# Function table loads written ahead of the wait of the activation that needs them

## The chip, the cores and the metric

The kernel runs on one core of a Trainium2 chip. The metric is the device time of one execution in microseconds; for a kernel run several times the median stands. The engines are TensorE (PE; its weight loads are PEld), VectorE (DVE), ScalarE (ACT), GpSimd (POOL) and SyncE (SP, which issues transfers).

## The reference

The reference is one forward pass of a hybrid network on an input of 2 x 512 x 128 elements read as 8 x 256 tokens of 128 channels. Sixteen blocks follow each other, each as `x = x + block(layernorm(x))`:

```
L0: selective scan,  experts (gelu, top 2 of 8),  linear attention (silu),  experts
L1: gated linear attention (sigmoid),  local attention + gelu MLP,  latent attention,  local attention + gelu MLP
L2: selective scan (silu),  experts (silu, top 2 of 8),  attention,  experts
L3: block-sparse attention,  slots,  grouped-query attention (two kinds),  slots
```

What matters for this change is which function each piece needs of ScalarE. Every layer norm needs `1/sqrt`, which the kernel computes as exp(-0.5 ln(v + eps)). Softmaxes need exp. The experts of L0 and the MLPs of L1 need gelu, the scan of L2, the experts of L2 and the linear attention need silu. The gated attention needs sigmoid. A slot block needs, in this order: ln and exp (norm), gelu, exp (softmax over the kept slots), sigmoid and tanh (the two gates and the candidate of a GRU cell), exp (a softmax between slots), ln and exp (norm).

## The kernel before

The 8 x 256 tokens are cut into four streams of 512 columns. Channels lie on the 128 partitions. Each stream runs all sixteen blocks in order, with its own quarter of the scratch space and its own two banks of PSUM; the streams depend on each other only at the start, at the weights' buffers and through the engines that they share.

The program has one instruction sequence per engine. What each stream does on an engine is a Python generator: `pe`, `act`, `dve`, `pool` and `sp` methods of the blocks. A generator yields the key of the event that its next piece waits for, on ScalarE with the function that the piece needs (for instance `yield self["gates"], ACT.Sigmoid`). It is resumed when `Core.run` (line 479) picks it; then it writes the wait and the instructions up to its next yield, and the events it posts get a semaphore count and a modelled time.

`Core.run` is a list scheduler. Each engine has a modelled time `free` at which it is done with what was written so far. Of all generators whose event has been posted, the one with the lowest rank goes next. The rank is a pair: the modelled start, and the event's time. On ScalarE a generator that needs another function table than the modelled one is ranked 500 ns later (`PATIENCE`, line 251), by `Scalar.delay` (line 333). `keep_clock` (line 503) puts extra matmuls into modelled gaps of TensorE. So every modelled time has a say in the order of the instructions on all engines; the order is fixed when the program is built.

A ScalarE function that isn't in the loaded table needs a table load (ACT_TABLE_LOAD in the trace). `Scalar.activation` (line 337) keeps the modelled table: Ln and Exp count as one, every other function as one of its own, and Copy, Identity and Square are in all. Where the modelled table becomes that of Ln and Exp, the kernel writes the load itself at line 342, directly in front of the activation, so behind the wait that was written before it. For all other functions the kernel writes none: the compiler puts in a load directly in front of an activation whose function isn't in the loaded table, and the trace shows it with the activation's line, 346. A wait may be a field of the instruction that waits, or an instruction of its own in front of it.

Some pieces name the function at the first of two waits. In the experts' silu step (lines 1426 to 1429):

```
e.wait_ge(*(yield self["up", i], ACT.Silu))
if i >= 2:
    e.wait_ge(*(yield self["down", i - 2]))
e.activation(self.h[i % 2][:, 0:width], self.a[:, 0:width], ACT.Silu).then_inc(...)
```

The same form stands at lines 1732 to 1735 (attention, Exp) and 2258 to 2261 (grouped-query attention, Exp). The slot block's ScalarE part is lines 2884 to 2912; its gates are at 2895 to 2898:

```
e.wait_ge(*(yield self["gates"], ACT.Sigmoid))
e.activation(gi[:, 0:2, :], gi[:, 0:2, :], ACT.Sigmoid).then_inc(*self.post("slot", "sigmoid"))
e.wait_ge(*(yield self["slot", "candidate"], ACT.Tanh))
e.activation(self.new, self.tmp, ACT.Tanh).then_inc(*self.post("slot", "tanh"))
```

Of the kernel before, what the change touches and what calls it, by code (L numbers as in the profile page):

```python
# [10 lines left out]
ACT = mybir.ActivationFunctionType  # L11
# [226 lines left out]
def cols(ap):  # L238
    return int(np.prod(ap.shape[1:]))
# [11 lines left out]
PATIENCE = 500  # L251
# [3 lines left out]
class Engine:  # L255
# [11 lines left out]
    def delay(self, function):  # L267
        return 0.0


class Tensor(Engine):

# [51 lines left out]

class Scalar(Engine):
    table = None
    LN_EXP, LN_EXP_TABLE, SWITCH = (ACT.Ln, ACT.Exp), 6, 1300
    IN_EVERY_TABLE = (ACT.Copy, ACT.Identity, ACT.Square)

    def table_of(self, function):  # L330
        return self.LN_EXP if function in self.LN_EXP else function

    def delay(self, function):
        other = function not in self.IN_EVERY_TABLE and self.table_of(function) != self.table
        return PATIENCE if function is not None and other else 0.0

    def activation(self, out, src, function, **kw):
        if function not in self.IN_EVERY_TABLE and self.table_of(function) != self.table:
            self.table = self.table_of(function)
            self.free += self.SWITCH  # L340
            if self.table == self.LN_EXP:
                self.engine.add_instruction(mybir.InstLoadActFuncSet(  # L342
                    name=self.nc.get_next_instruction_name(), act_func_set_id=self.LN_EXP_TABLE))
        self.free += 130 + 0.833 * cols(out) + 200 * ("accum_out" in kw)
        self.free += 90 * sum(k in kw and not isinstance(kw[k], float) for k in ("bias", "scale"))
        return self.engine.activation(out, src, function, **kw)  # L346


class Vector(Engine):
# [41 lines left out]
    def max(self, out, src):  # L391
        self.spend(src)
        return self.engine.max(out, src)
# [54 lines left out]
class Core:  # L448
# [30 lines left out]
    def run(self, programs):  # L479
        going = list(programs)  # L480
        for p in list(going):
            self.step(p, going)
        while going:
            best = None
            for p in going:
                if p.inner or (p.key is not None and p.key not in self.value):
                    continue
                e = self.engines[p.engine]
                at = self.value[p.key][2] if p.key is not None else e.free
                rank = max(e.free, at) + e.delay(p.function), at  # L490
                if best is None or rank < best[0]:
                    best = rank, p
            assert best is not None, [(p.engine, p.key) for p in going if not p.inner]
            rank, p = best
            if p.engine == "pe" and rank[0] > self.engines["pe"].free:
                self.keep_clock(rank[0], going)
            if p.key is not None:
                sem, value, at = self.value[p.key]
                p.got = sem, value
                self.engines[p.engine].free = max(self.engines[p.engine].free, at)  # L500
            self.step(p, going)
# [2648 lines left out]
```

## Time and profile before

| | us |
|---|---|
| median of 3 runs | 3782.72 |
| lowest, highest | 3773.63, 3789.63 |
| profiled execution, first to last instruction (span) | 3839.4 |
| TensorE busy (matmuls) in it | 3190.0 |
| VectorE busy | 2567.4 |
| ScalarE busy | 2219.9 |
| GpSimd busy | 1501.4 |

The profile is of one execution and gives its span; no time outside the span is given for it. Busy time is the time in which an engine executes an instruction, waits left out. The chain of waits follows the work that ended last back to what released it, step by step. A group of instructions shows its count, its busy time, the mean duration of one, the idle time of the engine directly before its instructions, and what ended that idle time.

### The profile page before, as it was taken

The page shows a single profiled execution, that of the slowest core. Times are in us where ns is not written, and L with a number is a line of the kernel's source. Part 1 is how long each engine was busy: PE and PEld are TensorE (multiplying, and loading weights), DVE is VectorE, ACT ScalarE, POOL GpSimd, SP SyncE. Part 2 cuts the span into 40 slices and gives each one's busy share as a digit, 9 for nine tenths or more (in the row PEclk, how much of TensorE's full clock was granted, in tenths as well). Part 3 has the DMA queues.
Part 4 walks back from the last instruction along what each step waited for, and adds up shares of the span by engine and source line. Part 5 has one row for each costly group of instructions (what it writes and reads, how often), then busy time and mean ns, then how long its engine had stood idle before and what let it go on. Part 6 is the DMA issues. An engine that isn't in the chain of part 4 may idle for free. (4 is left out here: it accounts for less than half of the span.)

```text
span 3839.4 us, 53645 instructions
## 1 busy us (share of the span) xinstructions
PE 3190.0 (83%) x18995; PEld 1876.0 (49%) x18995; DVE 2567.4 (67%) x6180; ACT 2219.9 (58%) x4841; POOL 1501.4 (39%) x1308
## 2 busy tenths in 40 slices
PE   3667788999889898988989878787887878898987
PEld 1234446755654554545455333454655647545434
DVE  3787975466778877676777899788444454556544
ACT  2445534542666776566766666574666746666653
POOL 1554654343543743214464575464222111211120
PEclk9788999999999999999999898898999988889987
DMA  5122212321210002210100001333334323331220
GB/s 204 44 80 62 80 54 89 94 68 38 81 33 1 1 5 61 49 36 20 48 1 1 31 31 34 102 96 99 114 87 127 95 77 121 101 87 25 49 49 6
DMA packets 193604, 238.34 MB, mean 62 GB/s; under 512 B 36984, under 2 KB 154168, under 8 KB 191288
## 3 DMA queue, kind: packets, MB, share of 16 engines
q1 hardware_dynamic: 169016, 157.43, 14.4%
q0 software_dynamic: 24320, 77.47, 6.5%
q8 instruction: 151, 2.47, 0.3%
q14 instruction: 117, 0.96, 0.1%
HBM read 183.61 MB, written 53.74 MB: 62 GB/s over the span
## 5 line engine op out<-in xcount | busy, mean ns | idle before, releaser
L346 ACT ACTIVATE scratch<-psum 128x512 f32<-128x512 f32 (+6 forms) x1812 | 841.0, 494 | 866.5 <-PE psum L306 627.4
L306 PE MATMUL psum<-scratch 128*128 128x128 f32 (+16 forms) x8016 | 962.0, 327 | 155.2 <-ACT scratch L346 44.8
L357 POOL TENSOR_TENSOR scratch<-scratch 128x512 f32<-128x512 f32 (+3 forms) x536 | 689.7, 1299 | 798.4 <-PE psum L306 240.5
L346 ACT ACTIVATE scratch<-scratch 128x255 f32<-128x255 f32 (+8 forms) x1368 | 620.0, 480 | 457.1 <-DVE scratch L369 214.2
L306 PEld LDWEIGHTS psum<-scratch 128*32 128x32 f32 (+9 forms) x8016 | 605.6, 149 | 551.1 <-issue 238.1
L306 PE MATMUL psum<-scratch,w_constants 128*128 128x512 f32 (+2 forms) x848 | 448.1, 621 | 25.8 <-ACT scratch L346 18.5
L369 DVE TENSOR_TENSOR_SCAN scratch<-scratch 128x512 f32<-128x512 f32 x256 | 416.3, 1627 | 33.0 <-POOL scratch L357 32.0
L357 DVE TENSOR_TENSOR scratch<-scratch,psum 128x512 f32<-128x512 f32 (+2 forms) x532 | 309.2, 586 | 166.3 <-PE psum L306 100.2
L322 PE MATMUL psum<-w_constants,scratch 128*128 128x128 f32 (+2 forms) x1880 | 322.4, 293 | 71.4 <-POOL scratch L357 29.4
L377 DVE TENSOR_REDUCE scratch<-psum 128x2 f32<-128x512 f32 (+2 forms) x336 | 224.9, 677 | 213.4 <-PE psum L306 182.3
L306 PE MATMUL psum<-scratch,w_early 128*128 128x256 f32 (+11 forms) x912 | 306.0, 473 | 64.2 <-DVE scratch L357 34.4
L322 PEld LDWEIGHTS psum<-w_constants,scratch 128*128 128x128 f32 (+2 forms) x1880 | 223.3, 143 | 203.4 <-issue 73.9
L424 POOL DMA_INDIRECT scratch<-L_experts_rows_dram,scratch x112 | 121.4, 1084 | 428.3 <-PE psum L306 336.0
L306 PE MATMUL psum<-scratch,w_local 128*128 128x128 f32 (+5 forms) x1064 | 270.8, 387 | 21.2 <-ACT scratch L346 14.1
L357 DVE TENSOR_TENSOR scratch<-psum,scratch 128x512 f32<-128x512 f32 (+4 forms) x456 | 212.2, 473 | 110.2 <-ACT scratch L346 73.5
L346 ACT ACT_TABLE_LOAD x194 | 248.9, 1283 | 40.8 <-PE psum L306 22.6
L306 PE MATMUL psum<-w_local,scratch 128*128 128x512 f32 (+3 forms) x608 | 254.0, 525 | 15.2 <-DVE scratch L373 9.0
L357 POOL TENSOR_TENSOR scratch<-scratch,xpos 128x512 f32<-128x512 f32 x128 | 174.9, 1371 | 219.7 <-DVE scratch L357 217.7
L357 DVE TENSOR_TENSOR scratch<-scratch 128x32 f32<-128x32 f32 (+14 forms) x488 | 210.6, 436 | 69.7 <-ACT scratch L346 61.7
L342 ACT ACT_TABLE_LOAD x162 | 207.8, 1283 | 65.9 <-PE psum L306 40.2
L306 PE MATMUL psum<-bf_masks 128*128 128x512 bf16 x643 | 217.7, 419 | 18.4 <-DVE scratch L357 11.3
L306 PEld LDWEIGHTS psum<-scratch,w_early 128*128 128x128 f32 (+6 forms) x912 | 135.7, 185 | 184.6 <-issue 80.6
(106 smaller groups left out, 4270.8 us busy)
## 6 DMA issues: line engine op xcount, KB each, us to landing
scratch<-b_out SPq DMA_DIRECT2D x80, 384.0 KB
slots_out<-scratch SPq DMA_DIRECT2D x112, 128.0 KB, 1.9
q_stack<-scratch SPq DMA_DIRECT2D x72, 192.0 KB, 2.6
scratch<-q_out SPq DMA_DIRECT2D x96, 96.0 KB
scratch<-slots_in SPq DMA_DIRECT2D x16, 512.0 KB
q_out<-scratch SPq DMA_DIRECT2D x40, 192.0 KB, 3.0
scratch<-slots_in SPq DMA_DIRECT2D x16, 448.0 KB
scratch<-q_stack SPq DMA_DIRECT2D x24, 288.0 KB
```

Of the source, the lines that this page charges most:

```text
L306: return self.engine.matmul(out, lhsT, rhs, start=start, stop=stop, **kw)
L322: return self.engine.transpose(out, src, ident)
L342: self.engine.add_instruction(mybir.InstLoadActFuncSet(name=self.nc.get_next_instruction_name(), act_func_set_id=self.LN_EXP_TABLE))
L346: return self.engine.activation(out, src, function, **kw)
L357: return self.engine.tensor_tensor(out, a, b, op)
L369: return self.engine.tensor_tensor_scan(out, *args)
L377: return self.engine.tensor_reduce(out, src, axis, op, **kw)
L424: return self.engine.indirect_dma_start(out, out_offset, src, in_offset)
```

## The change

Function tables get numbers, and there is one place that writes a load. `Scalar.prepare` compares the function's table with the modelled one; where they differ it notes the new table, adds 1300 ns to the modelled time and writes the load. It is called for the picked generator before its event's time is applied and before its wait is written (in `Core.run`), and once more in `Scalar.activation`, where it writes a load only if the table is still another one. The loads that the compiler wrote for Gelu, Silu, Sigmoid and Tanh are now written by the kernel. The rank of a generator that needs another table changes from max(free, at) + 500 ns to max(free + 500 ns, at). Waits, activations, transfers and the 500 ns stay.

```diff
 class Engine:
+    def prepare(self, function):
+        pass
...
 class Scalar(Engine):
     table = None
-    LN_EXP, LN_EXP_TABLE, SWITCH = (ACT.Ln, ACT.Exp), 6, 1300
+    SWITCH = 1300
     IN_EVERY_TABLE = (ACT.Copy, ACT.Identity, ACT.Square)
-
-    def table_of(self, function):
-        return self.LN_EXP if function in self.LN_EXP else function
+    TABLES = {ACT.Exp: 6, ACT.Ln: 6, ACT.Gelu: 10, ACT.Silu: 18, ACT.Sigmoid: 2, ACT.Tanh: 0}
+
+    def other(self, function):
+        return function not in self.IN_EVERY_TABLE and self.TABLES[function] != self.table
 
     def delay(self, function):
-        other = function not in self.IN_EVERY_TABLE and self.table_of(function) != self.table
-        return PATIENCE if function is not None and other else 0.0
+        return PATIENCE if function is not None and self.other(function) else 0.0
+
+    def prepare(self, function):
+
+        if function is not None and self.other(function):
+            self.table = self.TABLES[function]
+            self.free += self.SWITCH
+            self.engine.add_instruction(mybir.InstLoadActFuncSet(
+                name=self.nc.get_next_instruction_name(), act_func_set_id=self.table))
 
     def activation(self, out, src, function, **kw):
-        if function not in self.IN_EVERY_TABLE and self.table_of(function) != self.table:
-            self.table = self.table_of(function)
-            self.free += self.SWITCH
-            if self.table == self.LN_EXP:
-                self.engine.add_instruction(mybir.InstLoadActFuncSet(
-                    name=self.nc.get_next_instruction_name(), act_func_set_id=self.LN_EXP_TABLE))
+        self.prepare(function)
...
                 at = self.value[p.key][2] if p.key is not None else e.free
-                rank = max(e.free, at) + e.delay(p.function), at
+                rank = max(e.free + e.delay(p.function), at), at
...
             if p.engine == "pe" and rank[0] > self.engines["pe"].free:
                 self.keep_clock(rank[0], going)
+            self.engines[p.engine].prepare(p.function)
             if p.key is not None:
                 sem, value, at = self.value[p.key]
                 p.got = sem, value
                 self.engines[p.engine].free = max(self.engines[p.engine].free, at)
```

## Rows read from the trace of the kernel before

**Rows 1.** The page: totals, and busy tenths of two engines in 40 slices.

```profile
PE 3190.0 (83%) x18995; PEld 1876.0 (49%) x18995; DVE 2567.4 (67%) x6180; ACT 2219.9 (58%) x4841; POOL 1501.4 (39%) x1308
...
PE   3667788999889898988989878787887878898987
...
ACT  2445534542666776566766666574666746666653
```

**Rows 2.** The chain of waits: shares by line, and its earliest long piece.

```profile
by line: PE psum L306 18.1%; ACT scratch L346 4.6%; issue 3.1%; DVE scratch L357 2.3%; ACT L342 1.7%; PE psum L322 1.7%; another core or an unknown queue 1.0%; DVE scratch L377 0.9%; ACT L346 0.9%; POOL scratch L357 0.8%; DVE scratch L369 0
...
2373.90 2.59 PE psum L306 x16
```

**Rows 3.** Load groups, 2373.9 to 3839.4 (count | busy, mean ns | idle before).

```profile
L346 ACT ACT_TABLE_LOAD x105 | 134.7, 1283 | 13.0 <-PE psum L306 9.7 <-issue 1.6
L342 ACT ACT_TABLE_LOAD x101 | 129.6, 1283 | 35.1 <-PE psum L306 20.5 <-DVE scratch L369 8.7 <-DMA scratch<-k_stack 2.4
```

**Rows 4.** Groups on ScalarE, whole span: the loads.

```profile
L346 ACT ACT_TABLE_LOAD x194 | 248.9, 1283 | 40.8 <-PE psum L306 22.6 <-DMA scratch<-masks_dram 11.8 <-DVE scratch L357 1.6
...
L342 ACT ACT_TABLE_LOAD x162 | 207.8, 1283 | 65.9 <-PE psum L306 40.2 <-DVE scratch L369 10.2 <-DVE scratch L357 4.1
```

**Rows 5.** ScalarE timeline (start, us, instruction, [idle before]): two loads of line 342.

```profile
34.05 1.28 ACT L342 ACT_TABLE_LOAD   x1 [2.15 <-PE psum L306]
35.35 0.69 ACT L346 ACTIVATE scratch<-psum,w_constants 128x512 f32<-128x512 f32 x1
...
801.78 1.28 ACT L342 ACT_TABLE_LOAD   x1 [6.90 <-PE psum L306]
803.08 0.69 ACT L346 ACTIVATE scratch<-psum,w_constants 128x512 f32<-128x512 f32 x1
```

**Rows 6.** ScalarE's timeline, 486 to 494: loads of line 346.

```profile
486.69 0.60 ACT L346 ACTIVATE scratch<-psum 128x512 f32<-128x512 f32 x1
487.31 1.28 ACT L346 ACT_TABLE_LOAD   x1
489.77 0.63 ACT L346 ACTIVATE scratch<-scratch 128x512 f32<-128x512 f32 x1 [1.18 <-DVE scratch L357]
491.70 1.28 ACT L346 ACT_TABLE_LOAD   x1 [1.31 <-PE psum L306]
493.00 0.60 ACT L346 ACTIVATE scratch<-psum 128x512 f32<-128x512 f32 x1
```

**Rows 7.** ScalarE's waits (waiting <- ended by: us, times, longest).

```profile
ACT L342 <- PE psum L306: 40.2, 36, 6.9
...
ACT L346 <- DMA scratch<-masks_dram: 11.8, 1, 11.8
```

**Rows 8.** ScalarE's timeline, the last slot layer of the last stream.

```profile
3810.08 0.60 ACT L346 ACTIVATE scratch<-psum 128x512 f32<-128x512 f32 x1 [4.72 <-PE psum L306]
3810.69 1.28 ACT L346 ACT_TABLE_LOAD   x1
3814.83 0.42 ACT L346 ACTIVATE scratch<-scratch 128x256 f32<-128x256 f32 x1 [2.86 <-DVE scratch L357]
3816.02 0.31 ACT L346 ACTIVATE scratch<-scratch 128x128 f32<-128x128 f32 x1 [0.77 <-DVE scratch L357]
...
3820.24 1.28 ACT L342 ACT_TABLE_LOAD   x1 [1.03 <-DVE scratch L361]
```

**Rows 9.** Groups on ScalarE, 2700 to 2800: the loads.

```profile
L346 ACT ACT_TABLE_LOAD x14 | 18.0, 1283 | 0.3
L342 ACT ACT_TABLE_LOAD x14 | 18.0, 1283 | 5.7 <-PE psum L306 5.5
```

**Rows 10.** Busy time by stretch, each engine (instructions), granted clock and transfers.

```profile
1200.00:2000.00 800.00, 723.15 (x4581) 398.71 (x4579) 583.45 (x1720) 523.62 (x1525) 352.62 (x342) 0.96 0.09 27
2500.00:3300.00 800.00, 671.00 (x4624) 461.12 (x4624) 440.99 (x1034) 502.60 (x872) 234.20 (x211) 0.91 0.35 100
```

## The prediction

> **What bounds the kernel now.** I read the page's totals first: TensorE is busy for 83% of the span, ScalarE for 58% [rows 1]. The slices beside them show no stretch in which ScalarE is full (most are 4 to 7 tenths), while TensorE stands at 7 to 9 tenths from the fifth slice on. So ScalarE is not the bound as an engine; it matters as a link in the dependence chains of four streams. The chain of waits comes next: it was followed back to 2373.9 us only, so its shares are those of the last 1465.5 us. In it TensorE's matmul line has 18.1% of the span, and function table loads have 1.7% (line 342) and 0.9% (line 346 without a tile, which can only be loads) [rows 2]. That is 2.6% of 3839.4 us, or 100 us. The same stretch has 206 loads of 1.283 us, 264.3 us together [rows 3], so 100 / 264.3 = 0.38 of the load time in it lies on the chain. I use 0.38 as the price of a microsecond of load anywhere; the stretch before is assumed to be like it, since the chain is not shown there.
>
> Then the loads themselves. There are 356: 162 written by the kernel at line 342, all for the Ln/Exp table, and 194 put in by the compiler, recorded at line 346 [rows 4]. The two kinds treat the wait differently. At line 342 the wait stands in front of the load: ScalarE sat idle for 6.90 us at 801.78, then loaded for 1.28 us, and only then did the activation start [rows 5]. At line 346 a load often runs ahead of the wait already: at 487.31 the load follows the last activation at once, ends at 488.59, and the activation starts at 489.77 after 1.18 us more of idling [rows 6]. But not always: in the same rows the load at 491.70 had 1.31 us of idling in front of it. So about half of what the change says it does is done in the kernel before, and the gain is to be found in the idle time directly in front of loads.
>
> **The hiding of loads.** That idle time is 65.9 us for line 342 and 40.8 us for line 346 [rows 4]. Of the latter, 11.8 us are the program's first load, which waits for the masks' transfer; it belongs to a Copy, and Copy prepares nothing, so it stays where it is [rows 7]. 94.9 us remain. A load can win no more than its own 1.283 us, and 20 of the idle times are longer. Taken load by load from ScalarE's timeline, 75 of the 356 loads start after more than 0.06 us of idling; the first (after the masks) is the one at 34.05 with 2.15 us and the last the one at 3820.24 with 1.03 us [rows 5, 8]. With each cut at 1.283 us, the 74 without the masks' sum to 58.3 us: 43.7 at line 342 and 14.6 at line 346. The other 281 start within 0.06 us of the previous activation's end, where ScalarE itself is the late one: moving a load ahead of its wait gains nothing there. Bounds of this part: 0 (something else is late each time, mostly TensorE, which ended 40.2 us of the 65.9 us at line 342 and has its own queue [rows 7]) and -58.3 us (all of them on the path). I take 58.3 x 0.38 = **-22 us**. What becomes late next, where a load is hidden, is what the activation waited for in the first place: 34.05 [rows 5] waits for a matmul's result and then runs 1.28 us earlier.
>
> **Tanh gets a table of its own.** The new table of numbers gives Sigmoid 2 and Tanh 0, so each Tanh behind a Sigmoid asks for a load. The last slot layer shows none in the kernel before: Sigmoid (128x256) at 3814.83, then Tanh (128x128) at 3816.02 after 0.77 us of idling, with no load between [rows 8]. The layer occurs twice in four streams, so 8 loads are added. With the 0.77 us as cover, 1.28 - 0.77 = 0.51 us is exposed; without cover 1.28 us. 8 loads cost 4.1 to 10.3 us of ScalarE time; in the last stream, where nothing else runs, one is exposed by 0.51 us for certain, and the Exp load at 3820.24 gives back 1.03 us. At share 0.38 to 1 the eight cost 1.6 to 10.3 us; near the low end, since most have other streams beside them: **+3 us**. The Trainium skill ("ScalarE: Activation LUTs", "Table sets: the hidden batching unit") lists tanh as a member of the sigmoid set, and so speaks against this number in the change; by that rule, the trace agrees, a second load is pure cost. The same page ("What ACT_TABLE_LOAD costs") adds a drain of about 1.38 us to each load; if that were so and could be hidden too, an estimate of the hiding would be 94.9 x 0.38 = -36 us. The trace doesn't show one: a load starts in the same hundredths in which the previous activation ends and the activation follows it by 0.02 us [rows 6], so I price a load at 1.283 us and no more.
>
> **The new rank.** Before, a program that needs another table was ranked at max(free, at) + 500 ns; now at max(free + 500, at). The two agree when ScalarE is busy. They differ where it is idle, and then the switching activation may go up to 0.5 us earlier than it did, in front of another stream's activation that needs no switch. ScalarE's idle before the load shows that in about 75 places. ScalarE has some 4485 activations and reads in 3839 us, one in 0.86 us, so in 0.5 / 0.86 = 58% of these, some 43, another activation would have been first. Most such exchanges swap two neighbours and cost nothing. Some split a batch: the table goes away and must come back, two loads more. Bounds: none split, and the 43 switching activations are earlier by up to 0.5 us, 43 x 0.5 x 0.38 = -8 us; all split, 86 loads x 1.283 x 0.38 = +42 us. The rows are nearer to the lower end, since in the stretch with the densest switching, 2700 to 2800, ScalarE idles only 5.7 us before the 14 loads of line 342 and 0.3 us before the 14 others [rows 9]: there it is mostly busy, and the two ranks agree. I take one split in about nine, 10 loads: 10 x 1.283 x 0.38 = **+5 us**. The order of all other engines' work is derived from the same list, so it changes in many places with no sign that rows could give.
>
> Nothing else is added: no DMA, no semaphore, no activation. The load in front of a wait holds up nothing that it didn't hold up before, as the queue behind it was already behind the wait.
>
> **Sum.** -22 + 3 + 5 = -14 us on the profiled execution's 3839.4 us, which is its span; no time around it is given. That execution is 1.5% above the median of the runs, 3782.7 us. -14 / 3839.4 = -0.37%, so 3782.7 becomes **3769 us**. What a measurement of this kernel can tell from no change is about 0.5%, or 19 us: the forecast case lies close to that edge. Its own range is 3750 to 3783 us.
>
> **Rivals.** (1) *Slower by switches.* The place is the stretch 2500 to 3300, where experts' Silu and attention's Exp of different streams alternate: 28 loads in 100 us at 2700 [rows 9], with ScalarE busy 503 of 800 us [rows 10]. Two things there breed loads. The split batch is the first. The second is that some steps name the function at the first of two waits (Silu at line 1426, with the wait for the earlier block at 1428; Exp at 1732, with the values' wait behind): now the load is written at the first, and if another stream takes ScalarE for another table before the second, the load was for nothing and is written again. Each extra load costs 1.283 x 0.38 = 0.49 us. Without any, the case stands at -19 us; it decides from 19 / 0.49 = 39 extra loads, beside Tanh's 8 (403 in all), and is slower by 0.5% from 78 (442 in all). With 120 extra the time is 3782.7 - 19 + 58 = about 3822 us. For it: runs of one or two activations between loads are already common [rows 6]. Against it: the patience of 500 ns is kept wherever ScalarE is busy. The Trainium skill's rule on the same page, to batch calls by set and not by function, points to this case; by that rule, the trace agrees that each change of set is a load [rows 9]. (2) *Faster than the chain says.* The four streams take turns on the chain, and a load hidden off it shortens the next one; the whole 58 us comes, less Tanh's: 3782.7 - 55 = 3728 us. For it: the chain is spread thinly over all engines; against it: TensorE's 671 of 800 us busy in the densest stretch and 723 of 800 in 1200 to 2000 [rows 10]. (3) *Nothing comes of it.* Half of the loads were ahead of their waits anyway, and TensorE takes back what is won: 3783 us.
>
> **Chances.** Forecast case 0.45, (1) 0.25, (2) 0.15, (3) 0.15. Reordering adds some 20 us of either sign to each of them. Faster by over 0.5% (under 3764): 0.19 of the forecast case, nearly all of (2), a little of (3): 0.37. Slower by over 0.5% (over 3802): 0.21 of (1), 0.02 of the forecast case and 0.02 of (3): 0.25. Within: 0.38. Range 3717 to 3832: from below (2) to above (1).
>
> **What would show it.** Right: next to no idle time in front of loads (106.7 us now, line 346 and 342 together; 12 to 20 left), idle time behind them instead; all loads but the first at one line; 356 + 8 + about 10 loads; in the tail, a load between Sigmoid and Tanh and the Exp load ahead of its wait at the end. Wrong: over 400 loads with a longer time (rival 1); loads hidden and the span unchanged, with TensorE's waits on ScalarE unchanged (rival 3); or a gain over 40 us, which the loads in front of waits on the chain can't give alone.

## The result and the profile after

The changed kernel takes 3740.95 us (median of 4 runs, 3728.36 to 3743.47) beside 3778.18 us for the kernel before on the same chip (4 runs). The ratio is 0.9895, 95% interval 0.9862 to 0.9927. Two further comparisons on other chips gave 0.9875 (0.9849 to 0.9901) and 0.9877 (0.9857 to 0.9898). So the change takes off 1.05 to 1.25%, 37 to 53 us.

The totals of the profile after, and the busy tenths of TensorE and ScalarE (compare [rows 1]):

```profile
PE 3142.1 (84%) x18864; PEld 1849.7 (49%) x18971; DVE 2568.4 (69%) x6180; ACT 2208.1 (59%) x4834; POOL 1510.4 (40%) x1308
...
PE   3667788988789889989889967887898988888987
...
ACT  2445544654466676657667656584374857766754
```

ScalarE is busy for 12 us less. TensorE's busy time is 48 us less, but most of that need not be the change's: this trace holds 18864 matmuls beside 18971 weight loads, where the two counts are equal before, so 107 matmul records are missing. The traces of order_only (18971 matmul records) and order_only_2 (18864), one and the same program below, differ by 41 us. The span, 3737.7 us, is 101.7 us shorter than the one of before. This is more than the change is worth: the profiled executions of one and the same program can be 72 us apart on two chips (order_only and order_only_2: 3835.1 and 3763.1 us). Sizes in this document are therefore taken from ratios measured on one chip, and profiles are read for where things stand, not for how long the whole took.

The load groups of ScalarE, whole span (compare [rows 4]; line 345 is the new place where a load is written, line 352 the activation's):

```profile
L345 ACT ACT_TABLE_LOAD x348 | 446.5, 1283 | 27.6 <-PE psum L309 18.2 <-DVE scratch L363 3.5
...
L352 ACT ACT_TABLE_LOAD x1 | 1.3, 1283 | 11.8 <-DMA scratch<-masks_dram 11.8
```

349 loads in place of 356. The idle time in front of them, without the masks', is 27.6 us where it was 94.9 us. The chain of waits, shares of the span by line, now followed back over the whole span (compare [rows 2]):

```profile
by line: PE psum L309 43.6%; ACT scratch L352 8.4%; issue 7.9%; DVE scratch L363 7.1%; PE psum L325 4.7%; ACT L345 4.0%; DVE scratch L375 3.8%; DVE scratch L383 2.7%; POOL scratch L363 2.5%; POOL slots_in L430 1.9%; POOL scratch L430 1.7%; 
```

Loads have 4.0% of 3737.7 us, 150 us of the 448 us that 349 loads take: a share of 0.33 on the chain, where 0.38 had been read for the kernel before, from its last 1466 us alone.

The last slot layer of the last stream, on ScalarE (compare [rows 8]):

```profile
3705.09 0.60 ACT L352 ACTIVATE scratch<-psum 128x512 f32<-128x512 f32 x1 [1.22 <-PE psum L309]
3705.70 1.28 ACT L345 ACT_TABLE_LOAD   x1
3712.71 0.42 ACT L352 ACTIVATE scratch<-scratch 128x256 f32<-128x256 f32 x1 [5.72 <-DVE scratch L363]
3713.14 1.28 ACT L345 ACT_TABLE_LOAD   x1
3714.43 0.31 ACT L352 ACTIVATE scratch<-scratch 128x128 f32<-128x128 f32 x1
3717.92 0.61 ACT L352 ACTIVATE scratch<-psum,w_early 32x128 f32<-32x128 f32 x2 [3.17 <-PE psum L309]
3718.55 1.28 ACT L345 ACT_TABLE_LOAD   x1
3719.84 0.51 ACT L352 ACTIVATE scratch<-psum,scratch 64x64 f32<-64x64 f32 x2
```

Three things are to be seen. The Sigmoid's load (3705.70) ran ahead of its wait before and still does. A load stands between Sigmoid (128x256) and Tanh (128x128): Tanh starts 1.30 us after Sigmoid's end, and started 0.77 us after it before. The load for Exp (3718.55) now follows the last activation at once. Before, ScalarE waited for 1.03 us and loaded then; now the load takes 1.28 us and the wait is over when it ends, so the Exp starts 1.31 us behind the last activation where it was 2.33 us. Tanh costs this block 0.53 us and the Exp load gives back 1.02 us.

27.6 us of idling are left, in front of 16 loads, because a piece may have an earlier wait that names no function. The Gelu of the slot block waits for the hidden layer's bias before the step that names Gelu, and the load stands behind that first wait. Three of the 16 are of this kind, with 3.5 us. Twelve, with 17.7 us, stand in front of an activation of 128x512 that reads PSUM; the last Silu of a scan has that shape and, in the changed kernel's lines 790 to 792, the same two waits, so it is the likely one for most of them. From the changed kernel's timeline, a slot block:

```profile
3692.45 1.28 ACT L345 ACT_TABLE_LOAD   x1 [1.78 <-DVE scratch L363]
3694.09 0.68 ACT L352 ACTIVATE scratch<-psum,scratch 64x512 f32<-64x512 f32 x1 [0.36 <-PE psum L309]
```

### The profile page after: what moved, and what is told of

Read it like the earlier page. It is cut to its first block, busy times and chain, and to the rows that moved or that the text cites. A ratio compares the mean times of both kernels' runs of the same rounds, so it can differ in the third digit from the quotient of the medians.

```text
span 3737.7 us, 53437 instructions
## 1 busy us (share of the span) xinstructions
PE 3142.1 (84%) x18864; PEld 1849.7 (49%) x18971; DVE 2568.4 (69%) x6180; ACT 2208.1 (59%) x4834; POOL 1510.4 (40%) x1308
## 4 chain that ended last, share of the span: by engine, by line
PE 48%; DVE 21%; ACT 13%; issue 8%; POOL 6%; DMA 3%; SPq 1%; DVEq 0%; POOLq 0%; ACTq 0%
PE psum L309 44%; ACT scratch L352 8%; DVE scratch L363 7%; PE psum L325 5%; ACT L345 4%; DVE scratch L375 4%; DVE scratch L383 3%; POOL scratch L363 2%; POOL slots_in L430 2%; POOL scratch L430 2%; DVE scratch L367 2%; DVE scratch L371 1%; DVE scratch L379 1%; DVE scratch L387 1%; SPq L443 1%
## 5 line engine op out<-in xcount | busy, mean ns | idle before, releaser
L352 ACT ACTIVATE scratch<-psum 128x512 f32<-128x512 f32 (+9 forms) x1812 | 839.4, 494 | 848.5 <-PE psum L309 624.0
L309 PE MATMUL psum<-scratch 128*32 128x128 f32 (+14 forms) x8016 | 951.8, 327 | 129.0 <-ACT scratch L352 33.1
L352 ACT ACTIVATE scratch<-scratch 128x255 f32<-128x255 f32 (+9 forms) x1368 | 619.4, 479 | 473.3 <-DVE scratch L375 242.7
L345 ACT ACT_TABLE_LOAD x348 | 446.5, 1283 | 27.6 <-PE psum L309 18.2
L325 PE MATMUL psum<-w_constants,scratch 128*128 128x128 f32 (+1 forms) x1880 | 325.3, 295 | 72.3 <-POOL scratch L363 28.2
L309 PE MATMUL psum<-scratch,w_early 128*128 128x512 f32 (+11 forms) x912 | 292.6, 457 | 62.5 <-DVE scratch L363 41.9
L325 PEld LDWEIGHTS psum<-w_constants,scratch 128*128 128x128 f32 (+1 forms) x1880 | 227.0, 146 | 203.7 <-issue 76.8
L363 DVE TENSOR_TENSOR scratch<-psum,scratch 128x512 f32<-128x512 f32 (+3 forms) x456 | 212.6, 473 | 97.9 <-ACT scratch L352 74.4
L309 PE MATMUL psum<-w_local,scratch 128*128 128x512 f32 (+3 forms) x608 | 261.0, 538 | 22.2 <-DVE scratch L379 15.6
L363 DVE TENSOR_TENSOR scratch<-scratch 128x32 f32<-128x32 f32 (+12 forms) x488 | 211.5, 438 | 53.8 <-ACT scratch L352 42.8
L309 PE MATMUL psum<-scratch,bf_masks 96*128 96x256 bf16 (+3 forms) x480 | 121.1, 287 | 124.7 <-DVE scratch L363 106.6
L363 POOL TENSOR_TENSOR scratch<-scratch,bf_masks 128x512 f32<-128x512 f32 x64 | 76.1, 1191 | 327.4 <-ACT scratch L352 327.4
```

The lines of the kernel that those rows point to most:

```text
L309: return self.engine.matmul(out, lhsT, rhs, start=start, stop=stop, **kw)
L325: return self.engine.transpose(out, src, ident)
L345: self.engine.add_instruction(mybir.InstLoadActFuncSet(name=self.nc.get_next_instruction_name(), act_func_set_id=self.table))
L363: return self.engine.tensor_tensor(out, a, b, op)
```

## The experiments

Every kernel was compared with the kernel before on its own chip, and its ratio is always to that kernel, unless said otherwise. In "order of before" and "order of the changed kernel" below, the sequence of matmuls, activations, vector operations and transfers is that of the kernel before or of the changed kernel on every engine, instruction for instruction; only the loads differ. ScalarE's 4485 other instructions stand in the same order in the two traces of each pair. The diffs show the lines that matter; `...` stands for what is left out.

**Loads ahead of their waits, in the order of before (hide_only).** The modelled times and the rank are those of before; the load is written ahead of the wait, with a table of its own (`real`) kept beside the modelled one. `activation` calls `place` too, in place of the load that it wrote itself.

```diff
...
+    def place(self, function):
+        if function is not None and function not in self.IN_EVERY_TABLE and self.TABLES[function] != self.real:
+            self.real = self.TABLES[function]
+            self.engine.add_instruction(mybir.InstLoadActFuncSet(
+                name=self.nc.get_next_instruction_name(), act_func_set_id=self.real))
...
                 self.keep_clock(rank[0], going)
+            self.engines[p.engine].place(p.function)
             if p.key is not None:
```

> The order of every engine's work is the one of the kernel before, instruction for instruction; the function table loads are written where the change writes them, in front of the wait (360 loads, 4 of them for Tanh behind Sigmoid). Theory H (the gain is the hiding of loads): most of the 1.05% is here, about -20 to -40 us against before, and idle time in front of loads falls from 106.7 us to under 30. Theory O (the gain is the new order): -0 to -12 us. The forecast's term for hiding alone was -22 us, with +3 for Tanh.

Measured: 3829.01 us beside 3841.74 us, ratio 0.9965 (0.9946 to 0.9985), so -13 us, with -6 to -21 us in the interval. The idle time in front of loads fell as expected:

```profile
L345 ACT ACT_TABLE_LOAD x359 | 460.6, 1283 | 30.9 <-DVE scratch L378 10.3 <-PE psum L309 9.7 <-DVE scratch L366 4.9
```

Between 64 us less idling in front of loads and 13 us less time, most went to waits that ended when they did anyway. Three instructions that write x, the same three of the sequence in both kernels, show when the gain came (VectorE's timeline; first before, then hide_only):

```profile
1005.63 0.75 DVE L365 SCALAR_TENSOR_TENSOR x<-psum,w_early,x 128x512 f32<-128x512 f32 x1 [1.03 <-PE psum L306]
...
2441.27 2.20 DVE L357 TENSOR_TENSOR x<-x,scratch 128x512 f32<-128x512 f32 x1
...
3836.39 0.75 DVE L365 SCALAR_TENSOR_TENSOR x<-psum,w_early,x 128x512 f32<-128x512 f32 x1 [6.09 <-PE psum L306]
```

```profile
987.91 0.75 DVE L374 SCALAR_TENSOR_TENSOR x<-psum,w_early,x 128x512 f32<-128x512 f32 x1 [1.03 <-PE psum L309]
...
2427.11 2.20 DVE L366 TENSOR_TENSOR x<-x,scratch 128x512 f32<-128x512 f32 x1
...
3827.21 0.75 DVE L374 SCALAR_TENSOR_TENSOR x<-psum,w_early,x 128x512 f32<-128x512 f32 x1 [6.09 <-PE psum L309]
```

hide_only leads by 17.7 us at 1006 us, by 14.2 us at 2441 us and by 9.2 us at the end. One execution of each can't fix these to a few us, but the middle is plain: between 1200 and 2000 us there are hardly any loads (18 in the kernel before), and the lead doesn't grow from 1006 to 2441. The rest is not what a fixed price per load would give. These are the loads of the kernel before in the stretch 2500 to 3300, which has the most of them:

```profile
L346 ACT ACT_TABLE_LOAD x77 | 98.8, 1283 | 8.3 <-PE psum L306 7.0
L342 ACT ACT_TABLE_LOAD x75 | 96.2, 1283 | 29.2 <-PE psum L306 19.5 <-DVE scratch L369 7.7 <-DVE scratch L357 0.5
```

37.5 of the 94.9 us of idling stand there, about as much as before 1200 us (39.7 us), so the 100 us of [rows 9] are not typical of it. With each idle time cut at a load's 1.283 us, hide_only takes away 17 us of it in each of the two stretches. The lead grew to 18 us in the first; in the second it went from 14 us to at most 19 us, and 8 us of it were gone again between 3613 and 3783 us. The same hidden time was worth more in one stretch than in the other.

**The new order with loads placed as before (order_only).** Rank and modelled times are the changed kernel's. The loads of table 6 are written behind the wait, directly in front of the activation, the others are left to the compiler.

```diff
...
     def prepare(self, function):
         if function is not None and self.other(function):
             self.table = self.TABLES[function]
             self.free += self.SWITCH
-            self.engine.add_instruction(mybir.InstLoadActFuncSet(
-                name=self.nc.get_next_instruction_name(), act_func_set_id=self.table))
...
     def activation(self, out, src, function, **kw):
         self.prepare(function)
+        if function not in self.IN_EVERY_TABLE and self.TABLES[function] != self.real:
+            self.real = self.TABLES[function]
+            if self.real == 6:
+                self.engine.add_instruction(mybir.InstLoadActFuncSet(
+                    name=self.nc.get_next_instruction_name(), act_func_set_id=6))
```

> The order of every engine's work is the one of the changed kernel, instruction for instruction, but loads are placed as in the kernel before: those of the Ln/Exp table behind the wait, the others by the compiler (345 loads). Theory H: about the time of before, within 10 us. Theory O: most of the gain is kept, -25 to -40 us against before.

Measured: 3830.43 us beside 3841.74 us, ratio 0.9971 (0.9953 to 0.9988), -11 us. Neither theory got its way: placement on the old order, and the new order with the old placement, were each worth about a third of a per cent.

**All four cells on one chip (hide_only_2, order_only_2, after_3).** The product of the two, 0.9936, was short of the changed kernel's 0.9875 to 0.9895.

> Order of before, loads ahead of their waits, beside the other three cells on one chip. If hiding is worth the same on either order: 0.9965 again.

> Order of the changed kernel, loads placed as before, on the same chip. Theory A (placement and order add up, and the 0.9875 to 0.9895 of the changed kernel differ from the product 0.9936 by the chip): the product of this and the order of before with loads ahead equals the changed kernel's ratio within 0.2%. Theory M (hiding is worth more on the new order, some 0.9% in place of 0.35%): this stays at 0.997 and the changed kernel at 0.988.

> The changed kernel, on the same chip: 0.987 to 0.991 in both theories; it is the cell that the other two are compared with.

| | loads placed as before | loads ahead of the wait |
|---|---|---|
| order of before | 1 (3782.36 us) | 0.9965 (0.9942 to 0.9988), 3769.77 us |
| order of the changed kernel | 0.9961 (0.9946 to 0.9977), 3768.13 us | 0.9877 (0.9857 to 0.9898), 3738.01 us |

The load groups of order_only_2 (line 352: table 6; line 356: the compiler's), beside 27.8 us and the masks' 11.7 us in after_3:

```profile
L356 ACT ACT_TABLE_LOAD x189 | 242.5, 1283 | 54.4 <-PE psum L309 38.7 <-DMA scratch<-masks_dram 11.7 <-DVE scratch L367 0.9
L352 ACT ACT_TABLE_LOAD x156 | 200.1, 1283 | 58.5 <-PE psum L309 32.0 <-DVE scratch L391 14.8 <-DVE scratch L371 3.7
```

On the order of before, placement takes off 13 us; on the new one 3768.13 - 3738.01 = 30 us, 0.84%. The product of the single effects is 0.9926; the cell is 0.9877, and only the far ends of the intervals touch. Theory M is the likelier: the orders differ in how much of the hidden time reaches the end. From the means of the four cells' runs the difference is 15 us, with 4 to 24 us as its 95% interval (each cell's runs drawn anew at random, many times), so its size is loose. The idle time in front of loads is much the same in both (106.7 and 112.9 us, the masks' included), so the number that the profile gives beforehand doesn't tell the two apart. What in the new order makes the difference was not found, and these traces can't show it: the profiled execution of after_3 was the slowest of its five runs, and its span (3754.7 us) is only 8.4 us below that of order_only_2 (3763.1 us).

**The rank and the modelled charge, each taken back (old_rank, old_charge).** Loads are ahead of their waits in both. The charge is the place at which a load's 1300 ns enter the modelled time: before the event's time is applied in the changed kernel, after it in the kernel before. old_rank has the changed kernel's charge and the rank of before; old_charge has the new rank and the charge of before.

```diff
 # old_rank, on the changed kernel
-                rank = max(e.free + e.delay(p.function), at), at
+                rank = max(e.free, at) + e.delay(p.function), at
 # old_charge, on hide_only
-                rank = max(e.free, at) + e.delay(p.function), at
+                rank = max(e.free + e.delay(p.function), at), at
```

> The changed kernel with the old rank, max(free, at) + 500 ns; loads are ahead of their waits and the modelled time charges them there (377 loads, 28 more than the changed kernel). Theory H: as fast as the changed kernel or up to 28 x 0.49 = 14 us slower. Theory O with the rank as its cause: most of the gain is gone, within 10 us of before. If the charge is the cause: the gain stays.

> The changed kernel with the new rank and the loads ahead of their waits, but with the modelled time charging a load behind the wait, as before (373 loads). Theory H: a gain of 20 us or more. Theory O with the modelled charge as its cause: only the hiding's part, -5 to -12 us. With the rank as its cause: nearly the whole gain, -30 to -40 us.

Measured: old_rank 0.9990 (0.9972 to 1.0008), 3839.39 us; old_charge 1.0032 (1.0010 to 1.0055), 3852.22 us, both beside 3841.74 us. Each half alone, with all the hiding, is slower than hide_only (0.9965) and than the changed kernel. old_rank alone looks like Theory O with the rank as the cause: it is within 10 us of before. But by that theory old_charge, which has the new rank, should have kept nearly the whole gain, and it is slower than before with all the hiding in it. Read at face value the two say that rank and charge are only good together. The next two kernels say why it can't be read so.

**A change without direction (before_1283, after_1283).** The modelled load is 1283 ns in place of 1300 ns, in the kernel before and in the changed one: 17 ns in a figure that nothing but the order depends on. Below, a deal is one order that the scheduler comes out with.

```diff
-    LN_EXP, LN_EXP_TABLE, SWITCH = (ACT.Ln, ACT.Exp), 6, 1300
+    LN_EXP, LN_EXP_TABLE, SWITCH = (ACT.Ln, ACT.Exp), 6, 1283
```

> The kernel before with the modelled load at 1283 ns in place of 1300: a change with no sense or direction of its own, which only deals another order (381 loads, 25 more). It measures what a new deal of the order is worth. If orders scatter little, it is within 10 us of before; if the order's part of the gain is luck, it may differ by 10 to 30 us of either sign.

> The changed kernel with 1283 ns in place of 1300, another deal of the order under the new rules (367 loads, 18 more). If the new rules make better orders by themselves, it is about as fast as the changed kernel, within 10 us; if the changed kernel had a lucky deal, it falls back to the hiding's part, about -13 us against before.

Measured on one chip with after_again: before 3862.70 us, before_1283 3909.57 us, ratio 1.0136 (1.0110 to 1.0162); after_again 3809.46 us, after_1283 3947.28 us, ratio 1.0232 (1.0204 to 1.0259) to before and 1.0362 to after_again. 17 ns cost 47 us in the one and 138 us in the other. after_1283 is 85 us slower than before, far from both values that were set beside it: the new rules don't make good orders by themselves.

The two kernels are also a second pair of before and changed kernel, with the same edit between them. There the edit makes the kernel slower by 38 us, 1.0% (3947.28 beside 3909.57 us, and the intervals of the two ratios don't meet), where it is 1.2% faster at 1300 ns. So not only the size but the sign of the whole change depends on the deal. How the 38 us divide between the loads' placement and the order was not measured there.

A part of the loss is seen at the end. The last writes of x of the two streams that end last in before_1283 (VectorE's timeline):

```profile
3838.64 0.75 DVE L365 SCALAR_TENSOR_TENSOR x<-psum,w_early,x 128x512 f32<-128x512 f32 x1 [1.53 <-PE psum L306]
...
3912.85 0.75 DVE L365 SCALAR_TENSOR_TENSOR x<-psum,w_early,x 128x512 f32<-128x512 f32 x1 [6.09 <-PE psum L306]
```

The last stream runs alone for 74 us. In that time TensorE is busy for 60% at a granted clock of 0.54, near the lower of its two levels of 1.2 and 2.4 GHz. The stretches with the last stream alone in before_1283, after_1283, after_again and before, one line each (columns: stretch, length, busy time of PE, PEld, DVE, ACT, POOL with instructions, granted clock, busy share of the DMA engines, GB/s):

```profile
3839.00:3915.90 76.90, 46.02 (x184) 21.18 (x183) 21.34 (x74) 20.48 (x39) 4.61 (x4) 0.54 0.02 7
```

```profile
3866.00:3930.90 64.90, 37.74 (x128) 19.87 (x125) 17.88 (x63) 16.88 (x29) 1.15 (x1) 0.50 0.02 8
```

```profile
3794.00:3822.90 28.90, 13.69 (x48) 8.19 (x48) 7.30 (x26) 6.82 (x14) 0.00 (x0) 0.59 0.05 19
```

```profile
3815.50:3839.40 23.90, 12.80 (x45) 6.70 (x43) 5.00 (x16) 5.12 (x12) 0.00 (x0) 0.61 0.06 22
```

About 77, 65, 29 and 24 us. The lone stretch of before_1283 is 53 us longer than before's (whose profile is not from that comparison), as much as its whole loss of 47 us; of after_1283's 138 us over the changed kernel (same chip) it makes up 36, and the rest lies earlier.

**The changed kernel again, and without Tanh's loads (after_again, tanh_free).** tanh_free has the changed kernel's order and leaves out a load for Tanh when the table before it serves Tanh.

```diff
...
-            self.engine.add_instruction(mybir.InstLoadActFuncSet(
-                name=self.nc.get_next_instruction_name(), act_func_set_id=self.table))
+            if function != ACT.Tanh or self.real not in (0, 2, 10, 18):
+                self.real = self.table
+                self.engine.add_instruction(mybir.InstLoadActFuncSet(
+                    name=self.nc.get_next_instruction_name(), act_func_set_id=self.table))
```

> The changed kernel once more, beside the kernel before on the same chip. If placement (-0.35%) and order (-0.29%) add up, the ratio is 0.993 to 0.994; if they help each other, it is again 0.987 to 0.991.

> The changed kernel in the same order, without the loads for a Tanh whose table before it serves Tanh too: 345 loads in place of 349. By the forecast's term a Tanh load costs some 0.4 us each, so 4 fewer give -1.5 us, 0.04%, not to be told from the changed kernel; if the loads sit on the path in the last block, up to 5 us.

Measured: 0.9875 (0.9849 to 0.9901) and 0.9886 (0.9860 to 0.9913). The pair Sigmoid and Tanh in tanh_free's last block is 0.68 us apart and again without a load:

```profile
3782.18 0.42 ACT L355 ACTIVATE scratch<-scratch 128x256 f32<-128x256 f32 x1 [5.72 <-DVE scratch L366]
3783.28 0.31 ACT L355 ACTIVATE scratch<-scratch 128x128 f32<-128x128 f32 x1 [0.68 <-DVE scratch L366]
```

The 4 loads are worth nothing that can be measured. They are 4 and not 8 because the other four Tanhs have a load in the kernel before too. In all four another stream needed the Ln/Exp table between Sigmoid and Tanh. One of them, in the kernel before (ScalarE's timeline; Sigmoid is in the second line, with another activation merged behind it, Tanh in the last, and line 342 loads the Ln/Exp table between them):

```profile
3352.46 1.28 ACT L346 ACT_TABLE_LOAD   x1
3353.76 0.94 ACT L346 ACTIVATE scratch<-scratch 128x256 f32<-128x256 f32 x2
3354.71 1.28 ACT L342 ACT_TABLE_LOAD   x1
...
3357.85 1.28 ACT L346 ACT_TABLE_LOAD   x1
3359.14 0.31 ACT L346 ACTIVATE scratch<-scratch 128x128 f32<-128x128 f32 x1
```

Set side by side, order_only_2 and after_3 differ in the presence of a load at exactly four activations, all Tanhs. Tanh does not even need Sigmoid's table: the kernel before runs one behind a load that an activation of 128x384 (the width of the experts' Silu) had caused, and one, at 3519.17 us, behind the load of the slot block's Gelu. The first of the two (Tanh is the last line):

```profile
3235.41 1.28 ACT L346 ACT_TABLE_LOAD   x1
3236.70 0.87 ACT L346 ACTIVATE scratch<-psum 128x384 f32<-128x384 f32 x2
...
3239.96 0.30 ACT L346 ACTIVATE scratch<-scratch 128x128 f32<-128x128 f32 x1
```

**More patience (patience_1300).** The changed kernel with 1300 ns in place of 500 ns in the rank, to see whether fewer loads make it faster.

```diff
-PATIENCE = 500
+PATIENCE = 1300
```

> The changed kernel with a patience of 1300 ns in place of 500 ns in the rank: 229 loads, 120 fewer. At 0.49 us a load that is -59 us, so ratio 0.972 beside the changed kernel's 0.988. If the deal of the order outweighs it, as 17 ns in the modelled load did (+1.4% and +3.5%), anything from 0.96 to 1.02.

Measured: 3858.56 us beside 3782.36 us, ratio 1.0188 (1.0165 to 1.0210). It has 229 loads:

```profile
L345 ACT ACT_TABLE_LOAD x228 | 292.5, 1283 | 36.2 <-PE psum L309 19.1 <-DVE scratch L375 8.7 <-DVE scratch L363 3.1
```

120 loads fewer are 154 us of ScalarE's time, and the kernel is 120 us slower than the changed one. ScalarE's longest waits, in patience_1300 and in after_3 (us, times, longest):

```profile
ACT scratch L352 <- PE psum L309: 945.1, 855, 17.6
ACT scratch L352 <- DVE scratch L375: 262.8, 156, 12.2
```

```profile
ACT scratch L352 <- PE psum L309: 725.6, 664, 17.4
ACT scratch L352 <- DVE scratch L375: 253.2, 149, 7.8
```

The waits for matmuls' results are 220 us longer in total. ScalarE is busy for 141 us less and idle for longer by more than that: the time of the saved loads came back as waiting. Whether patience does that or only the deal of the order, one run of this kind can't say: 138 us is also what 17 ns did. No kernel tried beats the changed one by more than the measurement can tell.

## Why the prediction was right, and where it was not

It was 3769 us, 0.37% less, with a range of 3717 to 3832 us; measured were 3740.95 us, 1.05 to 1.25% less by ratio. The direction and the first mechanism hold. The size is a third of what was measured, "within 0.5%" had been given a hair more than "faster", and the time lies outside the forecast case's own 3750 to 3783 us: it is in the range because that reached down to rival 2. By two of the three comparisons (44 and 53 us) the gain is over 40 us, which the prediction had named as a sign that its account is wrong, and the experiments bear that sign out: the loads in front of waits don't give the gain alone. Of the signs for being right, all loads but the first are at one line, and the last block looks as described; but the idle time left is 39.4 us with the masks' and not 12 to 20, and there are 349 loads and not 374.

- *Half of the loads were ahead of their waits already; the gain is the idle time in front of the rest.* The second half is shown: the idle time fell from 94.9 us to 30.9 us with the order fixed, and the ratio was 0.9965 twice. "Half" is not so. Of the 356 loads of before, 19 (all of line 346) ran in idle time with more of it behind them, 75 started after a wait, and the other 262 had no wait beside them.
- *58.3 us x 0.38 = -22 us.* The size lies between the two that were measured, -13 us on the order of before and -30 us on the new one, and the first factor was too large. Cut at 1.283 us a load, 15.6 us of idling are still in front of 18 loads in hide_only, as they are in front of 16 in the changed kernel, so 42.7 us were hidden. 13 / 42.7 = 0.30, with 0.14 to 0.49 in the interval, so 0.38 is borne out as the price on a fixed order. On the new order it was 30 / 45.1 = 0.67. The price isn't a constant of the kernel: it depends on the order, and by the leads of hide_only on the stretch too. The side estimate of -36 us takes the 94.9 us uncut; with each idle time cut at 1.283 + 1.38 us, the load and the drain that it supposes, it would be an estimate of 74.8 x 0.38 = -28 us.
- *Tanh, +3 us for 8 loads.* 4 loads, no cost that can be measured. The cover of 0.77 us and the 0.51 us exposed behind it came as worked out (1.30 us less 0.77 us is 0.53 us), and the earlier Exp load gave back more. The count was wrong because it was taken from one block only, the one where nothing else runs; with other streams beside it, the Ln/Exp table came in between half of the time.
- *The new rank, +5 us from 10 extra loads.* The step that failed, by sign and by reasoning. With the charge it gave 7 loads fewer, Tanh's 4 included, and the new order alone was -11 to -14 us. The count of places where the two ranks differ was a way to price a single decision; but one decision changes all the later ones. It also leaned on [rows 9] for a ScalarE that is mostly busy where switching is densest, while 38 of the 74 loads that waited stand in 2500 to 3300. The two kernels with 17 ns show what the term was: a new deal, and those two came out 1.4% and 3.6% slower.
- *Reordering adds some 20 us of either sign.* Too small by far: 47 and 138 us. That the kernel came out faster owes much to the deal: of the seven orders that were measured, the changed kernel's is the fastest and that of before the second. Of the 1.2%, about a third of a per cent is the hiding on the order of before, a little more than a third the order, and the rest, of a size that these runs hold only loosely, appears with both.
- *Rival 1, slower by switches, from 39 extra loads at 0.49 us.* The price was wrong in both directions: 120 loads fewer came with +120 us (patience_1300), and before_1283 with 25 more loads lost 47 us, where 0.49 us each would be 12 us. The number of loads doesn't rank orders.
- *Rival 2, the whole 58 us.* Not on the order of before; with the new order 30 us came of the placement.

## What to carry to other kernels

Where an order of work is computed from modelled times, separate what an edit does to the instructions from what it does to the order: build the edit on the old order and the new order without the edit, and compare the four cells on one chip. Deal the order again with a change that means nothing (17 ns here), with and without the edit, before a gain is credited to a rule of the scheduler; this kernel moved by 1.4% and 3.6% from it, and the edit's 1.2% gain became a 1.0% loss. In front of such an edit, price the instruction's part by the idle time that the profile shows directly before the moved instruction, and give the order's part a range and no number.

## What had not been expected of the hardware

The same program in the same order (order_only and order_only_2) took 3835.1 us on one chip and 3763.1 us on another, 1.9% apart. The 72 us don't come evenly: at the same write of x the two are 12 us apart at 2683 us and 66 us at 3465 us. Why was not found. The kernel before had medians of 3778, 3842, 3863 and 3782 us in the four comparisons, so a time from one comparison can't be set beside one of another. A single stream alone kept TensorE busy for 60% of a stretch of 77 us, and its granted clock was 0.54 there, where it was 0.91 in the stretch 2500 to 3300 of the kernel before, with four streams.
